# Weight quantisation of a gated block moved from VectorE to GpSimd, filler products in two gaps of TensorE, and a new order of work, in a one-layer vision tower

## The reference

```python
h = tok(x, W, b)                                   # 768 -> 256
# recurrent block, on layernorm(h)
k = xk @ Wk.T; v = xv @ Wv.T; sr = sigmoid(xr @ Wr.T)
x = x + (sr * wkv(time_decay, time_first, k, v)) @ Wo.T
kk = square(relu(xk @ Wkey.T)); kv = kk @ Wval.T
x = x + sigmoid(xr @ Wrec.T) * kv
# gated block: weights in blocks of 32, 4 bits
s  = maximum(max(abs(wb), axis=-1) / 7, 1e-12)
wq = clip(round(wb / s), -8, 7) * s                # for w_gate, w_up, w_down
x = act_qdq(x); up = act_qdq(x @ wq_up.T); gate = act_qdq(x @ wq_gate.T)
o = act_qdq(act_qdq(gate * sigmoid_u16(gate)) * up)
return h + ... + o @ wq_down.T
```

## Time and profile before

| what | value |
|---|---|
| median of 3 runs | 154.41 us (154.13 to 154.87) |
| the profiled execution's own time | 154.9 us |
| its span in the trace | 153.1 us |
| TensorE busy | 124.0 us, 81% |
| VectorE busy | 120.8 us, 79% |
| ScalarE busy | 83.8 us, 55% |
| GpSimd busy | 22.8 us, 15% |
| mean granted clock of TensorE | 0.922 of full |

### The profile page before, as it was taken

The page is one execution under the profiler, slowest core; times in us unless marked ns, Lnnn a source line. Parts: engine busy times, 40 slices in busy tenths (PEclk is TensorE's granted clock), DMA queues, the critical chain, the costliest instruction groups (busy, mean ns, idle before and its releaser), DMA issues.

```text
span 153.1 us, 1841 instructions
## 1 busy us (share of the span) xinstructions
PE 124.0 (81%) x621; PEld 95.9 (63%) x621; DVE 120.8 (79%) x228; ACT 83.8 (55%) x160; POOL 22.8 (15%) x36
## 2 busy tenths in 40 slices
PE   7999989306984999999999997889999046628992
PEld 7867767104762777777777774668787036528881
DVE  0042698999899779789999769995579968999963
ACT  0312715975148478780577138836679597935300
POOL 3000000000000000000000000000059989750000
PEclk9999999975899599999999999999999855895999
DMA  5999991000000000000000000000000000000004
GB/s 155 344 371 421 423 413 51 0 0 0 4 2 0 0 2 0 0 0 4 0 0 0 0 0 0 4 0 2 0 4 0 0 0 0 0 0 0 0 4 154
DMA packets 4040, 9.03 MB, mean 59 GB/s; under 512 B 576, under 2 KB 2624, under 8 KB 3776
## 3 DMA queue, kind: packets, MB, share of 16 engines
q1 hardware_dynamic: 3024, 8.13, 13.9%
q10 hardware_dynamic: 1008, 0.80, 1.6%
HBM read 8.34 MB, written 0.59 MB: 58 GB/s over the span
## 4 chain that ended last, share of the span: by engine, by line
PE 57%; DVE 24%; POOL 7%; ACT 6%; issue 4%; DVEq 0%; POOLq 0%; ACTq 0%
PE ps L1072 19%; PE ps L1241 10%; PE ps L1163 4%; PE ps L1316 4%; PE ps L1317 4%; PE ps L1321 4%; PE ps L1090 4%; PE ps L1081 3%; POOL arena L315 3%; DVE mx L1014 3%; POOL arena L323 2%; DVE arena L1018 2%; POOL arena L328 2%; DVE ffn_lo L654 2%; PE ps L1166 1%
## 5 line engine op out<-in xcount | busy, mean ns | idle before, releaser
L315 POOL TENSOR_SCALAR arena<-arena,fac 128x576 int16<-128x576 f32 x5 | 5.9, 1179 | 71.9 <-DVE fac L937 71.9
L1072 PE MATMUL ps<-xk,wkey 128*128 128x288 f32 x64 | 16.0, 406 | 0.0
L1241 PE MATMUL ps<-front,wval 128*128 128x288 f32 x64 | 16.0, 406 | 0.0
L1163 PE MATMUL ps<-mean_w 128*128 128x128 f32 x66 | 12.3, 360 | 3.7 <-POOL arena L339 1.4
L559 ACT ACTIVATE arena<-ps,wrow 128x288 f32<-128x288 f32 x24 | 11.5, 498 | 5.8 <-PE ps L1321 5.8
L1072 PEld LDWEIGHTS ps<-xk,wkey 128*128 128x128 f32 x64 | 12.2, 191 | 3.5
L1163 PEld LDWEIGHTS ps<-mean_w 128*128 128x128 f32 x66 | 11.6, 268 | 4.5 <-POOL arena L339 1.8
L1241 PEld LDWEIGHTS ps<-front,wval 128*128 128x128 f32 x64 | 12.2, 190 | 3.4
L1316 PE MATMUL ps<-x_hi,ffn_hi 128*128 128x288 f16 x48 | 12.7, 286 | 0.6 <-DVE x_hi L955 0.6
L1317 PE MATMUL ps<-x_hi,ffn_lo 128*128 128x288 f16 x48 | 12.7, 286 | 0.0
L1072 PE MATMUL ps<-xk,wk 128*128 128x288 f32 x16 | 6.0, 540 | 7.7 <-DVE xk L707 7.7
(11 more groups left out here) (163 smaller groups left out, 317.4 us busy)
## 6 DMA issues: line engine op xcount, KB each, us to landing
wkey<-wkey_dram SPq DMA_DIRECT2D x1, 1024.0 KB, 11.0
wval<-wval_dram SPq DMA_DIRECT2D x1, 1024.0 KB, 12.8
front<-patches_dram SPq DMA_DIRECT2D x6, 144.0 KB, 4.1
front<-patches_dram SPq DMA_DIRECT2D x1, 864.0 KB, 7.0
front<-wtok_dram ACTq DMA_DIRECT2D x6, 128.0 KB, 4.5
ffn_raw<-wgate_dram SPq DMA_DIRECT2D x1, 768.0 KB, 9.1
ffn_raw<-wup_dram SPq DMA_DIRECT2D x1, 768.0 KB, 14.2
ffn_raw<-wdown_dram SPq DMA_DIRECT2D x1, 768.0 KB, 15.6
```

The source lines that it names most:

```text
L315: pool.tensor_scalar(dst[:, m, :], src[:, m, :], fac[:, i:i + 1], 0.0, ALU.mult, ALU.add)\
L1072: last = pe.matmul(dst, w[:, k, m * P:(m + 1) * P], src[:, c, k, :], start=(k == 0), stop=(k == blocks - 1))
L1163: pe.matmul(ps[:, b, 0:P], mean_w[:, :], mean_w[:, :], start=True, stop=True)
L1241: last = pe.matmul(bank(VALB[c] + m), wval[:, k, m * P:(m + 1) * P], hidden[:, k, c * CT:(c + 1) * CT], start=(k == 0), stop=(k == HK - 1))
```

## The change

1. **Weights of the gated block.** `round_weights` and `rescale` leave VectorE. GpSimd does them in four pieces of 128 x 384 each: the quotient (`tensor_tensor`), the rounding (`tensor_scalar` that adds and takes away 1.5 * 2^23, in float32) and the rescaling (`tensor_tensor`), which are 12 instructions per matrix and 36 in all. `block_maxima` and `block_scales` stay on VectorE and stand elsewhere. `weights` waits for four pieces where it waited for one.
2. **First column of the scan.** GpSimd's instruction before `maxima` is gone. The column is filled with a large negative number at the start, and `first_maxima`, two small VectorE instructions behind the scan, puts the right values in.
3. **Filler products.** `warm_wkv` puts 12 products ahead of `key_head(1)`, then 8 once `weight_state(0)` is done, then 8 once `denominator(0)` is done. `warm_mix` puts 7 ahead of `receptance(0)`.
4. **New order** on VectorE, ScalarE, TensorE and in SyncE's transfers (`wgate` goes ahead of `wk`, `wv` and `wr`).

```diff
-        wround_ready, wq_ready = sem("wround_ready"), sem("wq_ready")
+        wquot_ready, wround_ready, wq_ready = sem("wquot_ready"), sem("wround_ready"), sem("wq_ready")
...
             sp.dma_start(patches[:, 1, :, :], patches_d[:, 1, :, :]).then_inc(dma["in_patch1"], 16)
+            sp.dma_start(ffn_raw[:, 0, :], wgate_d).then_inc(dma["in_ffn0"], 16)
             sp.dma_start(wk[:, :, :], wk_d).then_inc(dma["in_wk"], 16)
...
+            pool.memset(kp[:, :, :, 0:1], NEG).then_inc(const_ready, 1)
...
-            pool.wait_ge(floor_ready, 1)
-            for c in range(CH):
-                pool.wait_ge(kp_ready, c + 1)
-                pool.tensor_tensor(kp[:, c, :, 0:1].rearrange("p (b i) t -> p b (i t)", b=FB),
...
+            def round_weights(i):
+                pool.wait_ge(binv_ready, i + 1)
+                for n in range(PREP):
+                    w3, blocks, shape = pieces(i, n)
+                    pool.tensor_tensor(w3, w3, binv[:, i, blocks].unsqueeze(2).to_broadcast(shape), ALU.mult)\
+                        .then_inc(wquot_ready, 1)
+                for n in range(PREP):
+                    w3, blocks, shape = pieces(i, n)
+                    pool.wait_ge(wquot_ready, PREP * i + n + 1)
+                    pool.tensor_scalar(w3, w3, RND, -RND, ALU.add, ALU.add).then_inc(wround_ready, 1)
+
+            def rescale(i):
+                pool.wait_ge(brel_ready, i + 1)
+                for n in range(PREP):
+                    w3, blocks, shape = pieces(i, n)
+                    pool.wait_ge(wround_ready, PREP * i + n + 1)
+                    pool.tensor_tensor(w3, w3, bmax[:, i, blocks].unsqueeze(2).to_broadcast(shape), ALU.mult)\
+                        .then_inc(wq_ready, 1)
+
+            for i in range(3):
+                round_weights(i)
+                rescale(i)
...
             def maxima(c):
                 dve.wait_ge(kp_ready, c + 1)
-                dve.wait_ge(first_ready, c + 1)
...
+            def first_maxima(c):
+                dve.wait_ge(pp_ready, c + 1)
+                for b in range(FB):
+                    s = slice(b * CI, (b + 1) * CI)
+                    dve.tensor_scalar(pp[:, c, s, 0:1], kp[:, c, s, 1:2], floor[:, b:b + 1], None, ALU.add)\
+                        .then_inc(first_ready, 1)
...
+            def warm_wkv():
+                warm(WARM_WKV[0], 6)
+                pe.wait_ge(weight_ready, 1)
+                warm(WARM_WKV[1], 6)
+                pe.wait_ge(den_ready, 1)
+                warm(WARM_WKV[2], 6)
+
+            def warm_mix():
+                pe.wait_ge(dev_ready, CH + 1)
+                warm(WARM_MIX, 4)
...
             channel_out(1)
-            rescale(2)
             deviation(2, 1)
```

More of the change, by code:

```diff
@@ L22 @@
 WARM = 9
+WARM_WKV = (12, 8, 8)
+WARM_MIX = 7
 WARM3 = 3
@@ L37 @@
 QB = 32
+PREP = 4
 ACT_SQ = (8, 7)
@@ L470, in _ @@
             rstd(0, 0)
+            embed(1, 0)
             affine(0, 0)
-            embed(1, 0)
             embed(1, 1)
+            centre_out()
+            square(0, 1)
             key_out(0)
-            square(0, 1)
             rstd(0, 1)
+            value_out(0)
+            affine(0, 1)
             exps01(0)
-            affine(0, 1)
-            value_out(0)
             gain_out(0)
+            soft_neg(0)
             soft_abs(0, 0)
@@ L483, in _ @@
             joint_log(0)
-            soft_neg(0)
+            key_out(1)
             sigmoid_out(0, 0)
-            centre_out()
-            key_out(1)
             square(1, 0)
             rstd(1, 0)
+            value_out(1)
             affine(1, 0)
             exps01(1)
+            gain_out(1)
             soft_abs(0, 1)
-            value_out(1)
-            gain_out(1)
             soft_neg(1)
+            soft_exp(0, 1)
             soft_abs(1, 0)
-            soft_exp(0, 1)
             relu(0, 0)
             relu(0, 1)
+            square_hidden(0, 0)
+            relu(0, 2)
             joint_log(1)
-            relu(0, 2)
             relu(0, 3)
+            square_hidden(0, 1)
             relu(0, 4)
@@ L836, in _ @@
             deviation(0, 0)
+            block_maxima(0)
+            block_scales(0)
             normalise(0, 0)
-            block_maxima(0)
+            out_centre()
             shift(0, 0)
             mix(0, 0, 0)
+            outer_norm(0)
+            deviation(0, 1)
             mix(0, 0, 1)
             mix(0, 0, 2)
-            out_centre()
-            deviation(0, 1)
             maxima(0)
-            outer_norm(0)
+            first_maxima(0)
+            normalise(0, 1)
             exponents(0)
-            normalise(0, 1)
             bonus_exponents(0)
+            shift(0, 1)
             weight_state(0)
-            shift(0, 1)
+            arrival(0)
             denominator(0)
-            arrival(0)
+            mix(0, 1, 0)
             joint(0)
             value_state(0)
-            mix(0, 1, 0)
+            mix(0, 1, 1)
             logsig(0, 0)
             numerator(0)
-            mix(0, 1, 1)
             rwkv(0)
+            maxima(1)
+            first_maxima(1)
+            residual(0)
             mix(0, 1, 2)
-            maxima(1)
-            residual(0)
-            block_maxima(1)
+            exponents(1)
+            normalise(1, 0)
             bonus_exponents(1)
-            normalise(1, 0)
-            exponents(1)
             shift(1, 0)
             mix(1, 0, 0)
+            mix(1, 0, 1)
             weight_state(1)
-            mix(1, 0, 1)
             denominator(1)
@@ L875, in _ @@
             value_state(1)
-            outer_norm(1)
             logsig(0, 1)
             numerator(1)
-            block_scales(0)
             rwkv(1)
-            round_weights(0)
+            outer_norm(1)
             residual(1)
             fold_squares(1, 1)
+            hx(0)
+            normalise(1, 1)
+            shift(1, 1)
+            row_scales(0)
+            mix(1, 1, 0)
             logsig(1, 0)
+            mix(1, 1, 1)
+            block_maxima(1)
             block_scales(1)
-            row_scales(0)
-            normalise(1, 1)
-            hx(0)
-            shift(1, 1)
-            mix(1, 1, 0)
-            hx(1)
-            mix(1, 1, 1)
-            channel_out(0)
-            block_maxima(2)
-            fold_tokens(0)
-            rescale(0)
+            block_maxima(2)
+            channel_out(0)
+            logsig(1, 1)
+            fold_tokens(0)
+            hx(1)
+            square_relu(1, 7)
             row_scales(1)
             deviation(2, 0)
-            round_weights(1)
+            fold_squares(2, 0)
             block_scales(2)
-            rescale(1)
-            fold_squares(2, 0)
-            square_relu(1, 7)
-            round_weights(2)
-            logsig(1, 1)
             row_scales(2)
             channel_out(1)
-            rescale(2)
             deviation(2, 1)
@@ L1262, in _ @@
             key_head(0)
-            value_head(0)
             var1()
             receptance_head(0, 0)
+            value_head(0)
             receptance_head(0, 1)
+            warm_wkv()
             key_head(1)
+            value_head(1)
             wkv_out(0)
+            half_var(1, 0)
             receptance_head(1, 0)
-            half_var(1, 0)
-            value_head(1)
             receptance_head(1, 1)
+            warm_mix()
             receptance(0)
@@ L1282, in _ @@
             keys(1, 0, 4)
+            keys(1, 4, 8)
             mean3_fold()
-            keys(1, 4, 8)
             values(1, 0, 0, 8)
             values(1, 1, 0, 8)
+            mean3(0)
+            weights(0, 1)
             var3_fold()
-            weights(0, 1)
-            mean3(0)
             mean3(1)
```

70 lines of the change are left out of this document (27 added, 43 removed).

## The result

The changed kernel takes 156.07 us (median of 20 runs) against 154.64 us for the one before (20 runs beside them on the same chips): a ratio of **1.0058, 95% interval 1.0035 to 1.008**. It is slower by a little over half a per cent, where 2.5 us less were forecast. Its profiled execution has a span of 154.4 us and an own time of 156.18 us.

The account below looks back on a forecast made before the run. VectorE bounds the kernel to 49.38 us, TensorE to 89.25, then VectorE, with clock falls second. Front -0.7, clock -1.9 and tail +0.15 sum to -2.5 us: 151.9 us against 154.41, range 149.9 to 155.2.

Parts of the forecast that it names:

- Part 2: Shared port in the front: GpSimd's pieces, 10 us a matrix, hold VectorE back 1.2 us; VectorE keeps the port between back-to-back instructions.
- Part 5: Tail, from the value products' end (T): one GpSimd piece in the way, first x_q at T + 9.65, 0.15 us later.
- three or four pieces between the maxima and the last x_lo: In the tail, GpSimd pieces at that place were listed as a sign that the forecast was wrong; no size given.
- rival of dearer pieces: GpSimd's pieces cost more through broadcasting a scale over 32 columns; from 1.1 us a piece the kernel takes 155.4 us; chance 0.12.
- The front: Up to `receptance(0)`: 1.9 us earlier with GpSimd's interference left out, 0.7 us earlier with it.
- Even, and I put it at 0: Fillers around `key_head(1)`: the 1.75 us they hold it back balances its faster run; 0, at most 0.3 us either way.
- Part 3: Fillers on TensorE keep the clock full, so `receptance(0)` takes 1.94 instead of 3.87 us: a gain of 1.9 us.
- the second rival: A fair port: GpSimd comes in between any two VectorE instructions; 154.5 us, no change; chance 0.16.
- Part 4: Squared-ReLU block: `mix(1, 1, 0)` ready 0.5 us early; 0 if VectorE keeps the port, otherwise 0.5 and 0.9 us more.
- The fillers ahead of `receptance(0)`: Seven filler products before that TensorE group keep the clock full there, worth 1.9 us.

Follow-up runs that it names:

- e4: The changed kernel with GpSimd's roundings in a different form for each matrix, to measure durations only; product and addition into int16 took 0.54 us; one run 153.8 us.
- after: The changed kernel itself, measured against the kernel before the change: 156.07 us, ratio 1.0058.
- e5: The changed kernel with 8 instead of 3 filler products ahead of the gate's first product: 155.09 us, ratio 1.0022 to the kernel before.
- e1: The changed kernel, but GpSimd starts the third matrix only when the last x_lo is written: 152.89 us, ratio 0.9858 to the kernel before.
- e3: The changed kernel without the fillers warm_wkv and warm_mix: 159.35 us, ratio 1.0229 to the kernel before.
- e6: e1 with GpSimd also starting the first matrix only when the recurrence of both chunks is done: 152.35 us, ratio 0.9857 to the kernel before.
- e7: e1 without warm_wkv, so only the 7 fillers of warm_mix ahead of the second receptance: 153.76 us, ratio 0.9943 to the kernel before.
- e10: The kernel before the change with both groups of fillers and one more wait: 153.23 us, against 154.92 us for the kernel before.
- e11: The changed kernel with quotient and rescaling back on VectorE in whole matrices, in the new order: 152.80 us, ratio 0.986 to the kernel before.

## Why the prediction was wrong

**The step that failed: the size of the rounding.** Part 2 says "a rounding is 0.74 x 384/576, 0.5". That 0.74 us was an instruction of another form, a product into int16. For that form the scaling was right: e4 measures 0.54 us. The change's rounding is two additions in f32, and takes 1.49 us at best in after and 1.69 on the mean. Thus the third matrix is not 10 us but 13.0. It also starts later, at T - 0.8 instead of T - 2, because the second matrix, with roundings as dear, keeps GpSimd until 87.26 us. So it ends 2.8 us behind the start of x_q instead of just over it. Part 5 put one piece in the way and 0.15 us; three were, and x_q to x_lo cost 1.75. The prediction's own list named this ("three or four pieces between the maxima and the last x_lo"), and its rival of dearer pieces gave 155.4 us, but for the wrong instruction, the broadcast of a scale: that one is 0.93 us and as forecast.

**A term that was missing: the clock behind the stall.** 1.6 us. e5 shows that it is a cost of its own, and e1 that without the stall it doesn't come. I looked for a clock fall only ahead of `receptance(0)`. What decides it isn't settled: e3 had the same waits and kept the clock. Three of after's 20 runs are 1.5 to 1.8 us quicker than the median, and their mean granted clock is 0.955 against 0.945 in the profiled one, so they kept it too. But three more, of 155.88 to 156.13 us, have 0.956 and aren't quicker; no trace of any of the six was taken, and what those three lost elsewhere is open.

**The front gave less, and for another reason.** 1.9 us earlier were forecast without interference; e6 has 1.2. Of these the 28 fillers, which I had put at 0, are 1.1 in the new order (e7) and 0.8 in the old (e10). The work taken off VectorE's path and the new order are then worth 0.1 to 0.4 us, in place of 1.9. One reason that fits is in e7: with the fillers gone TensorE runs its next two groups at half clock, 4.18 and 3.14 us, and a lighter VectorE only waits for it. The other is that `weight_state(0)` did come at 29.9 us in e6, as said, 0.5 later than before, so the gain had to come all behind it. There, from `weight_state(0)` to `receptance(0)`, it is 1.7 us with the fillers (20.05 before, 18.35 in e6). Which of the small terms fell short isn't settled. "Even, and I put it at 0" was the error on the fillers: I counted their hold on `key_head(1)` and the time it saves, and left out that the group behind it is quicker too. Part 3 also set unlike numbers side by side: 3.87 is the recorded length of `receptance(0)`, and 1.94 the time from one group's start to the next. From start to start the slow group is 53.08 - 49.38 = 3.70 us, so the clock there was worth 1.8 and not 1.9.

**The port: the number held, the rule behind it didn't.** With GpSimd at work, `weight_state(0)` came at 31.01 us (forecast 31.1) and the interference is 0.9 us (forecast 1.2). Part 2 had VectorE keep the port between instructions that follow each other. After's rows in the squared-ReLU block and the tail, VectorE and GpSimd:

```profile
68.09 1.51 DVE L715 SCALAR_TENSOR_TENSOR xr<-dm,vecs,hn 128x288 f32<-128x288 f32 x2
68.18 4.21 POOL L331 TENSOR_TENSOR ffn_raw<-ffn_raw,bmax 128x384 f32<-128x384 f32 x4 [40.69 <-DVE bmax L651]
...
94.43 0.75 DVE L699 TENSOR_TENSOR dev<-dev,lnr 128x576 f32<-128x576 f32 x1
```

Against GpSimd's two-operand pieces VectorE did not keep it. The two mixes at 68.09 us follow each other without a wait, and GpSimd's rescaling, at 68.18, comes in between: the first takes 0.51 us and the second 1.08, where before the pair took 0.95 (in 69.29 to 70.24 us). The pair at 70.20 us does the same. That is the fair port of the second rival, and TensorE felt only 0.19 us of it, since by Part 4's count that mix was 0.5 us early. Against the roundings there was hardly a port to keep. `normalise` at 94.43 us reads two operands from SBUF and takes its undisturbed 0.75 us, while one of GpSimd's roundings runs from 93.75 to 95.24 us and takes 1.50, undisturbed too. Between 21.54 and 23.73 us in the front, four VectorE instructions in a row likewise ran at their undisturbed lengths within GpSimd's roundings; the mix behind them took 0.75 us instead of 0.51, and the four roundings 7.63 us instead of 5.88. So Part 2's "waits for the other's whole instruction" fits the two-operand pieces and not these roundings, and that its 1.2 us came out near 0.9 is in part luck.

**What held.** The fillers ahead of `receptance(0)`: 1.7 us (1.9). `mix(1, 1, 0)`, which I put at 0 with 0.5 as its other end, cost 0.19 of waiting, and 0.5 with small things behind it. The deviation started at T + 2.2 (T + 2.0), and in e1, without GpSimd in the tail, the first x_q comes at T + 8.85 (T + 8.95).

**The sum put right.** With -0.3, -1.2, -0.2 and the rest's -0.7 as measured, and without the two terms of the third matrix, after would be 2.4 us quicker than before. e1 is that kernel, and is 2.4 us quicker in the medians and 2.3 in the span. That the two agree so well is partly chance, for e1's terms aren't quite these: T to x_q gives 0.65 instead of 0.2, and the rest only 0.1 instead of 0.7, since GpSimd's late conversion costs 0.6 there.

## What to carry to other kernels

When work is moved to an engine that shares a port, take its price from a row of the same operation form, not of the same engine and size; the form alone was nearly a factor of three here (1.49 to 0.51 us). Ask where the moved work ends in time, not only how long it takes, and keep its last pieces off the place where the next stage starts: waiting for that stage's last instruction gave 3.2 us. And try the fillers of TensorE alone first: in this kernel they were most of the gain (1.7 us in the medians, ratio 0.989), and the move of the arithmetic, the larger edit, brought little even at its best (e6 0.986, and e11 without it 0.986).
